# Moving four of sixteen row scalings, and the layer-two normalisation, from ScalarE to VectorE in a fused two-layer kernel

## The reference

```python
# layer one, for every window (t: 64 tokens x 128 channels)
tn = layernorm(t) * ln_g + ln_b
xi, z = split(tn @ W_in + b_in)               # 256 channels each
xc = silu(causal_conv4(xi) + conv_b)
dr, Bm, Cm = split(xc @ W_x)                  # 8, 16, 16
delta = softplus(dr @ dt_w + dt_b)
# for each of the 16 states n and every token:
#   h = exp(delta * A[:, n]) * h + (delta * xc) * Bm[:, n]
#   y += h * Cm[:, n]
out = ((y + xc * D) * silu(z)) @ W_out + b_out
x = out + x
# layer two
z = (x - mean) / sqrt(var + 1e-5) * gamma + beta     # over channels
# rfft2, 16 complex filters, irfft2, Theta, W1, gelu, W2, + x
```

## Time and profile before

| | |
|---|---|
| median of 3 runs | 9361.29 us (9360.03 to 9372.64) |
| the profiled execution, its own time | 9364.08 us |
| its span in the profile | 9362.3 us |
| granted TensorE clock, mean | 0.991 of full speed |
| `layer0` | from about 39 us to about 6,650 us |

### The profile page before, as it was taken

How to read it: one execution, slowest core, us unless ns; L and a number is a source line. 1 busy time by engine, 2 the same in 40 slices (tenths; PEclk the granted TensorE clock), 3 DMA queues, 4 the chain that set the end, 5 groups by cost and what they waited for, 6 DMA issues and landing times. The chain is left out here.

```text
span 9362.3 us, 162156 instructions
## 1 busy us (share of the span) xinstructions
PE 8641.8 (92%) x54525; PEld 6730.2 (72%) x54525; DVE 8300.9 (89%) x8144; ACT 7697.3 (82%) x13926; POOL 8064.1 (86%) x3865
## 2 busy tenths in 40 slices
PE   7999999999999999999999999999799999999899
PEld 4666666666666666666666666666688888888788
DVE  5999999999999999999999999999788888888766
ACT  6999999999999999999999999999555555555577
POOL 5999999999999999999999999999688888888500
PEclk8999999999999999999999999999899999999999
DMA  3333333333333333333333333333201001000265
GB/s 92 109 121 114 111 119 111 118 112 121 114 111 118 112 118 112 121 114 111 118 112 118 112 121 114 111 118 110 76 32 37 32 32 36 33 32 32 80 188 181
DMA packets 648481, 931.99 MB, mean 100 GB/s; under 512 B 79960, under 2 KB 277600, under 8 KB 643552
## 3 DMA queue, kind: packets, MB, share of 16 engines
q1 hardware_dynamic: 647904, 924.64, 31.4%
HBM read 778.38 MB, written 146.04 MB: 99 GB/s over the span
## 5 line engine op out<-in xcount | busy, mean ns | idle before, releaser
L1035 POOL TENSOR_TENSOR prod<-state,c_all 128x1024 f32<-128x1024 f32 x1280 | 3027.8, 2370 | 73.0 <-DVE state L909 72.9
L1024 POOL TENSOR_TENSOR drive_d<-du,b_all 128x1024 f32<-128x1024 f32 x1024 | 2424.2, 2367 | 9.4 <-issue 7.5
L909 DVE TENSOR_TENSOR_SCAN state<-decay_d,drive_d 128x1024 f32<-128x1024 f32 x1024 | 2336.6, 2282 | 77.1 <-ACT decay_d L724 77.1
L909 DVE TENSOR_TENSOR_SCAN state<-decay_r,drive_r 128x1024 f32<-128x1024 f32 x1024 | 2323.4, 2269 | 28.2 <-PE drive_r L581 17.5
L594 PEld LDWEIGHTS y_acc<-ident,prod 128*128 128x128 f32 x16384 | 1864.8, 142 | 632.1 <-issue 524.6
L594 PE MATMUL y_acc<-ident,prod 128*128 128x128 f32 x16384 | 2157.8, 276 | 43.1 <-POOL prod L1035 39.4
L1332 DVE SCALAR_TENSOR_TENSOR sum_d<-bank_d,filt,sum_d 128x512 f32<-128x512 f32 x2470 | 1666.6, 743 | 251.7 <-PE bank_d L1240 251.4
L737 ACT ACTIVATE ub<-ut,bt 128x256 f32<-128x256 f32 x4096 | 1739.1, 500 | 12.4 <-PE drive_r L581 12.0
L1379 POOL TENSOR_TENSOR sum_p<-sum_p,scaled 128x1024 f32<-128x1024 f32 x650 | 1553.4, 2390 | 210.9 <-ACT scaled L1290 173.6
L1290 ACT ACTIVATE scaled<-bank_p,filt 128x512 f32<-128x512 f32 x1560 | 945.4, 689 | 889.4 <-PE bank_p L1240 886.4
L724 ACT ACTIVATE decay_d<-delta,neg_a 128x504 f32<-128x504 f32 x2048 | 1312.1, 674 | 79.7 <-DVE state L909 78.7
(11 more groups left out here) (155 smaller groups left out, 14620.6 us busy)
## 6 DMA issues: line engine op xcount, KB each, us to landing
c_all<-bc_rows SPq DMA_DIRECT2D x1280, 256.0 KB, 3.3
b_all<-bc_rows SPq DMA_DIRECT2D x1024, 256.0 KB, 3.9
ys<-row_spectra SPq DMA_DIRECT2D x130, 256.0 KB, 2.8
column_sums<-tt SPq DMA_DIRECT2D x130, 256.0 KB, 2.1
x_in<-in_x_dram SPq DMA_DIRECT2D x64, 512.0 KB, 5.0
x_res<-in_x_dram SPq DMA_DIRECT2D x64, 512.0 KB, 5.0
x_rows<-x SPq DMA_DIRECT2D x64, 512.0 KB, 4.6
row_spectra<-z SPq DMA_DIRECT2D x64, 512.0 KB, 3.7
```

The source lines that it names most:

```text
L909: dve.tensor_tensor_scan(state[n % NT][:].rearrange("p h t -> p (h t)"), decay[:].rearrange("p h w t -> p (h w t)"), drive[:].rearrange("p ...
L1024: pool.tensor_tensor(drive_d[place_of(DSTEPS, n, ND)][:], du[:, :, q * HT:(q + 1) * HT], b_all[slot][:].unsqueeze(1).to_broadcast([P, 2, HT]),
L1035: pool.tensor_tensor(prod[n % NP][:], state[n % NT][:], c_all[slot][:].unsqueeze(1).to_broadcast([P, 2, HT]), ALU.mult).then_inc(s["prod_g ...
```

## The change

Four of the 16 odd steps of a block, steps 5, 11, 21 and 27, have their four scalings done by VectorE at the places h = 4, 16, 36 and 48, which are the same places in the order of steps (three steps ahead) as they had on ScalarE. All four parts of `make_z1` go to VectorE at their old places. Each is a `tensor_scalar` with the scalars read from a column, from SBUF to SBUF. TensorE waits on a semaphore of its own for each maker. The selection matrix shrinks from 48x16x128 to 48x16, and the matmul reads one column of it 128 times. The functions that work out buffer places take the block number too; with the rings as they are (4 or 2 buffers, and 12, 16, 20 and 32 steps) they give the same places as before, and `DSTEPS` and `BY_GPSIMD` are written out with the values that they had.

```diff
+UB_AT = {5: 4, 11: 16, 21: 36, 27: 48}
+Z1_BY_VECTOR = (0, 1, 2, 3)
-        "pick": sb("pick", [LOW + NS, NS, P], F32R),
+        "pick": sb("pick", [LOW + NS, NS], F32R),
-                                   base=-LOW * part, pattern=[[-1, NS], [0, P]],
+                                   base=-LOW * part, pattern=[[-1, NS]],
# TensorE
-                pe.matmul(c_bank[:], wt["pick"][:, n % NS, :], c_rows[q][:], start=True,
+                pe.matmul(c_bank[:], wt["pick"][:, n % NS:n % NS + 1].to_broadcast([LOW + NS, P]), c_rows[q][:], start=True,
-                need(pe, s["ub_done"], upto(RSTEPS, M, n))
+                if n in UB_AT:
+                    need(pe, s["ub_v_done"], upto(scaled_by(True), M, n))
+                else:
+                    need(pe, s["ub_done"], upto(scaled_by(False), M, n))
# ScalarE
-                    if h == AT["z1"][i] and S.tail:
+                    if h == AT["z1"][i] and S.tail and i not in Z1_BY_VECTOR:
                         make_z1(m, i)
-                    if (n + 3) % NSTEP in RSTEPS and S.step(n + 3, p):
+                    if (n + 3) % NSTEP in scaled_by(False) and S.step(n + 3, p):
# VectorE
+            def scale_u(S, step):
+                M, p, n = step
+                q, st = n // NS, n % NS
+                need(dve, s["drive_r_done"], upto(RSTEPS, *before_in(RSTEPS, M, n, NS_UB)))
+                if q == 0:
+                    taken(dve, S.last if M == S.m else S, "bt0", "ut00", "ut10")
+                else:
+                    taken(dve, S, "bt1", "ut01", "ut11")
+                for g in range(4):
+                    last = dve.tensor_scalar(ub[place_of(RSTEPS, M, n, NS_UB)][:, g, :], ut[q][:, g, :],
+                                             bt[q][:, g, st:st + 1], None, ALU.mult)
+                last.then_inc(s["ub_v_done"], 1)
+
+            def make_z1(m, i):
+                need(dve, s["yo_stored"], (m - 1) * 16)
+                need(dve, s["shift1_done"], m - 1)
+                for r in range(2 * i, 2 * i + 2):
+                    last = dve.tensor_scalar(z1[:, r, :], x1[:, r, :], rstd1[:, r:r + 1], shift1[:, r:r + 1],
+                                             ALU.mult, ALU.add)
+                last.then_inc(s["z1_v_done"], 1)
...
+                for i in Z1_BY_VECTOR:
+                    if h == AT["z1"][i] and S.tail:
+                        make_z1(m, i)
+                for n, place in UB_AT.items():
+                    if h == place and (S.scan if place <= 2 * n else S.front):
+                        scale_u(S, (m, p, n) if place <= 2 * n else (m + 1, f, n))
```

More of the change, by code:

```diff
@@ L57 @@
 LOW, DTR, BR = 32, 64, 72
-DSTEPS = tuple(n for n in range(NSTEP) if n % 2 == 0)
-RSTEPS = tuple(n for n in range(NSTEP) if n % 2 == 1)
+DSTEPS = (0, 2, 4, 6, 8, 10, 12, 14, 16, 18, 20, 22, 24, 26, 28, 30)
+RSTEPS = tuple(n for n in range(NSTEP) if n not in DSTEPS)
 ALLSTEPS = tuple(range(NSTEP))
-BY_GPSIMD = tuple(sorted(RSTEPS + (8, 12, 18, 20)))
+UB_AT = {5: 4, 11: 16, 21: 36, 27: 48}
+BY_GPSIMD = (1, 3, 5, 7, 8, 9, 11, 12, 13, 15, 17, 18, 19, 20, 21, 23, 25, 27, 29, 31)
 BY_VECTOR = tuple(n for n in ALLSTEPS if n not in BY_GPSIMD)
@@ L111, in upto, with scaled_by, place_of @@
     return M * len(steps) + nth(steps, n + 1)
-def place_of(steps, n, ring):
-    return nth(steps, n) % ring
+def scaled_by(vector):
+    return tuple(n for n in RSTEPS if (n in UB_AT) == vector)
+def place_of(steps, M, n, ring):
+    return (M * len(steps) + nth(steps, n)) % ring
 def before_in(steps, M, n, ring):
-    i, size = nth(steps, n), len(steps)
-    d = next(d for d in range(1, size + 1) if (i - d) % size % ring == i % ring)
-    return (M, steps[i - d]) if d <= i else (M - 1, steps[i - d + size])
+    i = M * len(steps) + nth(steps, n) - ring
+    return i // len(steps), steps[i % len(steps)]
 def nth_load(steps, M, n, ring):
-    i = nth(steps, n)
-    return M * sum(k % ring == i % ring for k in range(len(steps))) + i // ring + 1
+    return (M * len(steps) + nth(steps, n)) // ring + 1
 class Slot:
@@ L479, in scanned, with z1_made @@
             need(eng, s["scan_done"], M * NSTEP + n + 1)
+        def z1_made(eng, m, quarters):
+            by_v = len(Z1_BY_VECTOR)
+            done = sum(i < quarters for i in Z1_BY_VECTOR)
+            need(eng, s["z1_v_done"], m * by_v + done if done else 0)
+            need(eng, s["z1_done"], m * (4 - by_v) + quarters - done if quarters > done else 0)
         def multiplied(eng, M, n):
@@ L697, in body @@
                 for n in range(NSTEP):
-                    if n + 1 in RSTEPS and S.scan:
+                    if n + 1 in RSTEPS and n not in RSTEPS and S.scan:
                         turn_drive(S.step(n + 1, p))
@@ L884, in body @@
                         make_decay(S.step(n + 2, p))
-                    if (n + 3) % NSTEP in RSTEPS and S.step(n + 3, p):
-                        if (n + 3) % NSTEP == RSTEPS[0]:
+                    if (n + 3) % NSTEP in scaled_by(False) and S.step(n + 3, p):
+                        if (n + 3) % NSTEP == scaled_by(False)[0]:
                             taken(act, S, "bt0", "ut00", "ut10")
-                        if n + 3 == next(k for k in RSTEPS if k >= NS):
+                        if n + 3 == next(k for k in scaled_by(False) if k >= NS):
                             taken(act, S, "bt1", "ut01", "ut11")
@@ L902, in scan @@
                     need(dve, s["drive_d_done"], upto(DSTEPS, M, n))
-                    decay, drive = decay_d, drive_d[place_of(DSTEPS, n, ND)]
+                    decay, drive = decay_d, drive_d[place_of(DSTEPS, M, n, ND)]
                 else:
```

40 lines of the change are left out of this document (21 added, 19 removed).

## The result

| | before | changed |
|---|---|---|
| median | 9363.94 us (4 runs) | 10920.51 us (10917.76 to 10924.18, 4 runs) |
| ratio | 1 | 1.166 (95% interval 1.164 to 1.168) |
| span of the profiled execution | 9362.3 us | 10916.0 us |

The changed kernel is 16.6% slower. The forecast (9,335 us, the likeliest case) was wrong; the time lies 310 us above the 10,610 us that the first rival gave, and 270 us above the end of the wide range.

The account below looks back on a forecast made before the run. No single engine bounds it: four engines in fixed orders hold each other. VectorE loses 2.0 us a block, ScalarE gives back 2.4: -0.4, times 64 is -26 us, 9338 (median 9335); forecast range 9,270 to 9,420, 8 in 10 9,180 to 10,650.

Parts of the forecast that it names:

- the first rival: In layer0, VectorE scalings and GpSimd exclude each other: 18.4 us of waiting a block, about 10,610 us; chance 0.36.
- the wide range: Whole kernel: the 8-in-10 range for the time, 9,180 to 10,650 us.
- What comes to VectorE: In each block, 24 scalings at setup prices add 5.9 us to VectorE, bounds 1.4 to 9.2 us.
- The evidence for the two ports: Setup scalings of 128x1040 last 1.08 us against 1.21 for a PSUM product; rate agrees with ports shared with GpSimd.
- Where the cover lies: In a block, VectorE's idle time absorbs 1.9 us at h = 3 to 5 and 2.0 later; 2.0 us lost.
- What ScalarE gives back: In a block, earlier ScalarE shortens TensorE's 3.1 us and GpSimd's 4.5 us of waits; 2.4 us taken.
- The rest: Smaller `pick`, weight load, place arithmetic, DMA order and new waits count nothing; up to 0.5 us a block kept for range.
- The signs to watch: Profile signs in layer0: right, scalings about 0.35 us and ScalarE near 85% busy; collision, scalings of 1 us and more.

Follow-up runs that it names:

- The run with the load alone: Against the kernel before with only the smaller selection matrix: ScalarE keeps all scalings, VectorE does 16 extra bn_stats of 128x256 a block; 9600.31 us, ratio 1.025.
- the relief alone: Against the kernel before with only the smaller selection matrix: scalings of steps 5, 11, 21, 27 left out, done by no engine; 9316.91 us, ratio 0.995.
- two steps at h = 14 and 44: Changed kernel with only scalings of steps 9 and 25 on VectorE, at h = 14 and 44, rows normalised on ScalarE; 9458.27 us, ratio 1.010.
- normalisation alone: Changed kernel with only the normalisation of rows on VectorE (8 instructions a block), no scaling of delta*x; 10202.19 us, ratio 1.089.

## Why the prediction was wrong, by its own steps

- **What comes to VectorE** is the step that failed. It took the setup's 0.27 and 0.195 us, "since it is the same operation between the same memories", and its bounds stopped at 9.2 us a block; measured are 24.2 us. The undisturbed price was right: 2.19 us for eight. What was left out of the sum is that GpSimd was idle in the setup and works 94.6% of `layer0`. The bounds should have held the price beside a busy neighbour, which the first rival had.
- **The first rival** named the mechanism and nearly its size: 18.4 us of waiting a block, measured 24.2 - 5.9 = 18.3 us. That the size fits so well is in part luck: the sum put 3.5 us on each of seven places and took three quarters of it, while in the trace about 14 of the 24 instructions of a block wait, 1.25 us each on average. Its time came out 310 us too low because of the other term, 2.2 us of VectorE's other waits. These were to shrink from 7.0; they are 126.25 x (1 - 3744.75/4000) = 8.1 us (the rest of VectorE's work reads about 1.2 us lower and takes back a part). The largest, for the turned `y` that `gate` takes, went from 2.5 to 127.7/31.7 = 4.0 us: TensorE, held up by late scans, is late in its turn. I gave this rival 0.36 and not the first place for want of a row that shows the lock.
- **The evidence for the two ports** was read too broadly. The rows of 128x1040 give one column in about 1 ns (1.02 us for 1040), with `phi` read in a turned order, and show no doubled rate. What does is the step from 128x128 to 128x256 in the same rows: 0.27 - 0.195 = 0.075 us for 128 columns more, 0.6 ns a column, against 1,205/1024 = 1.2 ns for the product with an operand in PSUM.
- **Where the cover lies.** I counted 3.9 us of the 5.9 as absorbed by idle time. The run with the load alone adds 5.5 us and loses 3.7: 1.8 us are absorbed. Idle time in a coupled order is not spare time. Why the rest is not absorbed was not tested; I take it that most of it lies ahead of instructions whose inputs come through VectorE's own scans.
- **What ScalarE gives back**, 2.4 us, was mis-sized: 0.7 us with nothing added to VectorE (for the scalings alone), and nothing once VectorE is loaded. The profile's longest wait was for ScalarE's softplus, but in its queue ScalarE itself then waited for TensorE.
- **The rest** held: the selection matrix costs nothing, no idle time stands in front of the new instructions, GpSimd's products last as long as before (2,372 ns). The DMA queues were to keep their order; even so GpSimd now waits for a row of B, which it did not before, 21.7/31.7 = 0.7 us a block. The weight load, for which I kept up to 0.5 us, has the same 182 ns.
- **The signs to watch**: "scalings of 1 us and more in the view by line" is what the profile shows. ScalarE's busy share was to fall to 85% and is at 69% of the stretch (2771.91/4000), because the period grew.

Together, for the four steps of scalings: 3.7 us a block are VectorE's load, and the remaining 19.7 of 23.4 us come with the collision: 15.6 us directly (19.9 - 4.3), and some 4 us that I work out as the difference and did not test, most likely late scans handed on. TensorE's own busy time rose too, from 94.6 to 102.1 us a block in the changed kernel (3237.25/31.7), and its part in the 4 us is not separated. No version tried here beats the kernel before; the relief alone, without any price, would give 0.5%, so a better home for these scalings has little to win.

## What to carry to other kernels

Before work moves to VectorE, ask two things of each instruction: is it of a form that waits for GpSimd (here a scaling from SBUF to SBUF, or a product of two SBUF tiles; not bn_stats, a copy from PSUM, or a scan with an operand in PSUM), and what does GpSimd do at that moment? Beside a busy GpSimd each such instruction waits for the running one, now and then for two or three, so many short ones are the worst choice, fewer long ones cost less (6.8% in place of 16.0% here), and places where GpSimd waits are cheap. Whether a scaling with its input in PSUM would have been spared was not tried. A price taken from a quiet stretch of the profile holds for quiet stretches. And the engine that the others wait for is not the one to relieve until its own waits have been read.

## What was not expected of the hardware

- Beside ten products the two engines take turns, one scaling for one product (18.83 us for 8), and VectorE pays nearly all: 2.1 us for each scaling, against 43 ns for each product (2,382 against 2,339). In `layer0` the turns are not always fair: the longest scaling took 5,041 ns (two steps at h = 14 and 44) and the longest normalisation 6,483 ns (normalisation alone), more than two GpSimd instructions. GpSimd's products kept 2,372 ns in the changed kernel, against 2,370.
- The wait is inside the duration: VectorE looks 94% busy while it stands still. Of the views only the spread of durations (319 to 2,462 ns) shows it.
- bn_stats reads SBUF at 408 ns for 128x256 beside a busy GpSimd, with 418 ns as the longest of 1,024; copies from PSUM show no wait either (0.34 us each). Two inputs in SBUF wait as a scaling does (2.49 us each).
- The granted TensorE clock of the stretch fell from 1.00 (the 2.4 GHz level) to 0.91 (a mean over both levels) in the changed kernel, where TensorE is busy 81% and not 93%; the matmul that adds and turns a product there takes 284 ns against 275. I take this as a consequence of TensorE's waits; no run changes the clock alone.
